# Transformer layer on one core: the start of the attention re-ordered, query weights in two loads, a third weight buffer and later weight differences

## What is computed

```python
x = x + attention(layernorm(x))      # 32 heads of 16, 8 key/value heads
x = x + ffn(layernorm(x))            # 512 -> 1792 -> 512, silu(gate) * up
# bitnet_linear, for q, k, v and o:
s = maximum(mean(abs(weight), axis=1), 1e-8)
y = einsum('bsi,oi->bso', x, sign(weight / s[:, None])) * (s * scale_param)
# weights of the ffn (w1, w2, w3, each with its mean matrix):
d = w - base; W = base + mean(abs(d)) * sign(d)
```

## Time and profile before

| | us |
|---|---|
| median of three runs | 1043.14 |
| lowest and highest run | 1037.54, 1047.61 |
| the profiled execution, its own time | 1045.2 |
| its span, first to last instruction | 1043.4 |

### The profile page before, as it was taken

How to read it: one execution, slowest core, us unless ns; L and a number is a source line. 1 busy time by engine, 2 the same in 40 slices (tenths; PEclk the granted TensorE clock), 3 DMA queues, 4 the chain that set the end, 5 groups by cost and what they waited for, 6 DMA issues and landing times.

```text
span 1043.4 us, 14700 instructions
## 1 busy us (share of the span) xinstructions
PE 967.9 (93%) x4962; PEld 625.4 (60%) x4962; DVE 712.9 (68%) x946; ACT 553.3 (53%) x1078; POOL 301.7 (29%) x310
## 2 busy tenths in 40 slices
PE   6478989999989998898789999999999999999997
PEld 5233443344334433333457888888888888888886
DVE  4666878689978796685785558845686457864443
ACT  4436878888888887784673322233213232232231
POOL 3455537654665432324401110101101111111110
PEclk8768989999999998898999999999999999999999
DMA  5417557467645676632383000340003300220001
GB/s 181 136 26 207 149 146 198 146 195 186 201 121 157 186 190 180 201 98 83 103 291 127 1 1 1 106 141 0 0 0 123 123 0 0 69 93 0 0 0 41
DMA packets 77684, 109.74 MB, mean 105 GB/s; under 512 B 6720, under 2 KB 30272, under 8 KB 77632
## 3 DMA queue, kind: packets, MB, share of 16 engines
q1 hardware_dynamic: 76768, 108.09, 34.4%
q10 hardware_dynamic: 416, 0.66, 0.2%
q0 software_dynamic: 448, 0.33, 0.2%
HBM read 75.17 MB, written 32.77 MB: 103 GB/s over the span
## 4 chain that ended last, share of the span: by engine, by line
PE 72%; POOL 7%; DVE 5%; DMA 4%; issue 4%; SPq 4%; ACT 3%; ACTq 0%; DVEq 0%; POOLq 0%
PE psum L1597 15%; PE psum L1598 15%; PE psum L1599 15%; PE psum L1501 7%; PE psum L1491 6%; PE psum L1475 4%; PE psum L1395 3%; DMA stage<-in_L_ffn_mean_w_dram 2%; PE psum L1396 2%; POOL xn L693 2%; PE psum L1512 1%; PE psum L1513 1%; DVE stage L1309 1%; POOL stage L757 1%; DVE nmx L1147 1%
## 5 line engine op out<-in xcount | busy, mean ns | idle before, releaser
L1147 DVE TENSOR_REDUCE nmx<-psum 128x2 f32<-128x1024 f32 x256 | 305.0, 1221 | 84.9 <-PE psum L1475 82.5
L975 ACT ACTIVATE probs<-psum 128x512 f32<-128x512 f32 x512 | 270.6, 600 | 57.6 <-PE psum L1491 57.1
L1597 PE MATMUL psum<-fxh,wh 128*128 128x512 f32 x448 | 175.3, 391 | 2.2 <-DVE wl L1320 2.2
L837 POOL CAST dh<-w2T 128x512 fp32r<-128x512 f32 (+1 forms) x56 | 50.8, 909 | 430.7 <-PE psum L1599 393.6
L1598 PE MATMUL psum<-fxl,wh 128*128 128x512 f32 x448 | 175.0, 391 | 0.0
L1599 PE MATMUL psum<-fxh,wl 128*128 128x512 f32 x448 | 174.9, 391 | 0.0
L1491 PE MATMUL psum<-q_slot,k_slot 50*128 50x512 f32 x512 | 155.4, 485 | 18.1 <-ACT probs L975 13.7
L1491 PEld LDWEIGHTS psum<-q_slot,k_slot 50*128 50x128 f32 x512 | 67.4, 192 | 139.0 <-ACT probs L975 69.7
L1501 PE MATMUL psum<-probs,v_slot 128*32 128x512 f32 x1024 | 144.3, 637 | 0.0
L1327 DVE TENSOR_TENSOR gate<-gate,psum 128x512 f32<-128x512 f32 x56 | 38.4, 686 | 133.8 <-PE psum L1599 131.5
L1033 ACT ACTIVATE hh<-gate 128x512 fp32r<-128x512 f32 x56 | 35.4, 632 | 162.2 <-DVE gate L1327 162.2
(11 more groups left out here) (133 smaller groups left out, 1315.7 us busy)
## 6 DMA issues: line engine op xcount, KB each, us to landing
stage<-in_L_ffn_mean_w_dram SPq DMA_DIRECT2D x84, 256.0 KB, 4.4
q_slot<-q_stack SPq DMA_DIRECT2D x62, 192.0 KB, 3.3
stage<-in_L_ffn_w_dram SPq DMA_DIRECT2D x42, 256.0 KB, 5.2
q_stack<-q_hi SPq DMA_DIRECT2D x32, 256.0 KB
weighted_values<-u_sb SPq DMA_DIRECT2D x32, 256.0 KB, 3.9
k_slot<-k_stack SPq DMA_DIRECT2D x62, 96.0 KB, 3.6
q_stack<-q_lo SPq DMA_DIRECT2D x16, 256.0 KB
an<-weighted_values SPq DMA_DIRECT2D x16, 256.0 KB
```

Of the source, the lines that this page charges most:

```text
L837: nc.gpsimd.tensor_copy(dh[parity][:], w2T[:, bass.ds(src, 1), :].rearrange("p o c -> p (o c)")).then_inc(dh_ok, 1)
L975: nc.scalar.activation(probs[kt][:, j, :], BANK[ring_bank(("score", g, kt, j))], ACT.Exp, scale=HEAD_DIM ** -0.5).then_inc(exp_ok, 1)
L1147: v.tensor_reduce(column, pair, AX.X, ALU.max, negate=True).then_inc(s_max, 1)
L1597: mm(o, lhs_hi, rhs_hi, start=first, stop=False)
```

## The change

The tiles of K, V and Q are renumbered so that K, V and the first quarter of Q come together. The query weights arrive in two loads, the first quarter alone. The scales of K, V and that quarter are made at once. ACT's magnitudes and signs of the other quarters move behind the first items. PE multiplies the K item as each quarter of `xl` is ready. Twelve small loads of group 0 go over SP and ACT and six over POOL; before it was eight and ten. The third and fourth quarter of Q's pieces are placed one by one after plain scores 2 to 12, the four output sign tiles after 7 to 10. Tile 0 of the differences is loaded in the prologue, ahead of group 1. `stage` gets a fifth buffer, w uses three of the five and mean two, magnitudes overwrite w's buffer. Differences, statistics, `NORM_AT` and `ATTENDED_AT` shift by a few slices, `PROJECT_AT` comes two slices earlier, and five mean tiles are loaded ahead in the last five groups. Renamed indices and the unchanged body of `load_tile` are cut from the diff.

```diff
-QT, KTILE, VTILE, OT = 0, 4, 5, 6
+KTILE, VTILE, QT, OT = 0, 1, 2, 6
...
-LATER = (None, 3, 0, 0)
-XT_AT, SPLIT_AT, STATS_AT, AGGR_AT = 0, 1, 14, 18
-NORM_AT = (24, 26, 28, 30)
+LATER = (None, 2, 0, 0)
+XT_AT, SPLIT_AT, STATS_AT, AGGR_AT = 0, 1, 18, 22
+NORM_AT = (24, 25, 27, 28)
...
-SELECT_AT = (2, 7)
-INVERT_AT, ATTENDED_AT = 27, 9
-PROJECT_AT = (22, 24, 26, 28)
+SELECT_AT = (6, 11)
+INVERT_AT, ATTENDED_AT = 27, 12
+PROJECT_AT = (20, 22, 24, 26)
...
-DIFF_AT = tuple(range(5, 112, 8))
+DIFF_AT = tuple(range(8, 113, 8))
...
-RING = 4
+RING, RING_HERE = 5, 4
...
-    stage = [mid(f"stage{p}", [P, 3, HID]) for p in range(RING)]
-    wn, mn = stage[0::2], stage[1::2]
+    stage = [mid(f"stage{p}", [P, 3, HID]) for p in range(RING_HERE)]
...
-    mid("below_late", [P, 1280])
+    stage.append(mid("stage4", [P, 3, HID]))
+    wn, mn = stage[0::2], stage[1::2]
...
-    WEIGHT_SETS = ((KTILE, 2), (QT, 4), (OT, 4))
+    WEIGHT_SETS = ((KTILE, 3), (QT + 1, 3), (OT, 4))
...
-    FIRST_LOADS, FIRST_POOL = 8 * 16, 10 * 16
+    FIRST_LOADS, FIRST_POOL = 12 * 16, 6 * 16
...
-    TOTALS_SLICE, MEANS_SLICE, COEFF_SLICE = 119, 120, 121
+    TOTALS_SLICE, MEANS_SLICE, COEFF_SLICE = 121, 122, 123
...
-    def first_keys(eng, part):
+    def first_keys(eng, part, done):
...
-            eng.dma_start(k_slot[0][r:r + HEAD_DIM, :].bitcast(FP32), src[0:HEAD_DIM].bitcast(FP32)).then_inc(first_in, 16)
+            eng.dma_start(k_slot[0][r:r + HEAD_DIM, :].bitcast(FP32), src[0:HEAD_DIM].bitcast(FP32)).then_inc(done, 16)
...
+        def load_difference(e, part):
+            if part == 0:
+                if e >= 3:
+                    sp.wait_ge(facc_ok, 3 * (e - 2))
+                    sp.wait_ge(fsgn_ok, 3 * (e - 2))
+                load_tile(e, wn[e % 3], (w1, w3, w2), fw_in[e % 3])
+            else:
+                if e >= 2:
+                    sp.wait_ge(fd_ok, 3 * (e - 1))
+                load_tile(e, mn[e % 2], (m1, m3, m2), fw_in[e % 3])
...
-        sp.dma_start(w_nat[:, QT:QT + 4, :], q_w.rearrange("(t p) c -> p t c", p=P)).then_inc(w_in[1], 16)
+        sp.dma_start(w_nat[:, QT, :], q_w[0:P, :]).then_inc(w_in[1], 16)
+        sp.dma_start(w_nat[:, QT + 1:QT + 4, :], q_w.rearrange("(t p) c -> p t c", p=P)[:, 1:, :]).then_inc(w_in[2], 16)
...
-        sp.dma_start(w_nat[:, OT:, :], o_w.rearrange("(t p) c -> p t c", p=P)).then_inc(w_in[2], 16)
+        sp.dma_start(w_nat[:, OT:, :], o_w.rearrange("(t p) c -> p t c", p=P)).then_inc(w_in[3], 16)
...
+        sp.wait_ge(qh_ok, 1)
+        first_keys(sp, 1, slot_in[0])
+        first_keys(sp, 2, slot_in[0])
...
+        load_difference(0, 0)
+        load_difference(0, 1)
...
-        def load_difference(e, part):
-            if part == 0:
-                if e >= 2:
-                    sp.wait_ge(facc_ok, 3 * (e - 1))
-                    sp.wait_ge(fsgn_ok, 3 * (e - 1))
-                load_tile(e, wn[e % 2], (w1, w3, w2), fw_in[e % 2])
-            else:
-                load_tile(e, mn[e % 2], (m1, m3, m2), fw_in[e % 2])
...
-            if g == 0:
-                load_difference(0, 0)
-                load_difference(0, 1)
-            elif g % 2 == 1 and g // 2 + 1 < IT:
+            if g % 2 == 1 and g // 2 + 1 < IT:
...
-            elif g % 2 == 0 and g // 2 < IT:
+            elif 0 < g // 2 < IT and g % 2 == 0:
...
-            if g >= GROUPS - 4:
-                e = g - GROUPS + 4
-                sp.wait_ge(facc_ok, 3 * (IT - 1 + e // 2))
-                sp.wait_ge(fsgn_ok, 3 * (IT - 1 + e // 2))
+            if g >= GROUPS - RING:
+                e = (4, 1, 0, 3, 2)[g - GROUPS + RING]
+                last = (IT - 3, IT - 2, IT - 2, IT - 1, IT - 1)[g - GROUPS + RING]
+                if e in (1, 3):
+                    sp.wait_ge(fd_ok, 3 * (last + 1))
+                else:
+                    sp.wait_ge(facc_ok, 3 * (last + 1))
+                    sp.wait_ge(fsgn_ok, 3 * (last + 1))
...
-        pool.wait_ge(qh_ok, 1)
-        first_keys(nc.gpsimd, 1)
-        first_keys(nc.gpsimd, 2)
...
-        first_keys(nc.gpsimd, 0)
+        first_keys(nc.gpsimd, 0, first_in)
...
-        for part in range(2):
-            first_heads(nc.gpsimd, part, 1, first_in)
+        first_heads(nc.gpsimd, 1, 1, first_in)
+        pool.wait_ge(ql_ok, 2)
+        first_heads(nc.gpsimd, 2, 1, first_in)
+        for t in range(2):
+            norm_tokens(1, t)
...
+        norm_tokens(1, 2)
+        split_item(0, 3)
...
-        split_item(0, 3)
+        norm_tokens(1, 3)
...
-        for t in range(TT):
-            norm_tokens(1, t)
...
-                pool.wait_ge(fw_in[e % 2], 96 * (e // 2 + 1))
-            nc.gpsimd.tensor_tensor(wn[e % 2][:, k, :], wn[e % 2][:, k, :], mn[e % 2][:, k, :], ALU.subtract).then_inc(fd_ok, 1)
+                pool.wait_ge(fw_in[e % 3], 96 * (e // 3 + 1))
+            nc.gpsimd.tensor_tensor(wn[e % 3][:, k, :], wn[e % 3][:, k, :], mn[e % 2][:, k, :], ALU.subtract).then_inc(fd_ok, 1)
...
+        act.wait_ge(w_in[1], 16)
+        magnitude(QT)
...
-        for m in (KTILE, VTILE):
+        for m in (KTILE, VTILE, QT):
...
-        act.wait_ge(w_in[1], 16)
-        for m in range(QT, QT + 4):
-            magnitude(m)
-        for m in (KTILE, VTILE):
+        for m in (KTILE, VTILE, QT):
...
-        act.wait_ge(wstat_ok, 2)
-        sign_tile(QT)
...
-        signs_out(QT)
...
-        sign_tile(QT + 1)
+        act.wait_ge(w_in[2], 16)
+        magnitude(QT + 1)
+        magnitude(QT + 2)
...
-        sign_tile(QT + 2)
+        magnitude(QT + 3)
...
+        act.wait_ge(qh_ok, 2)
+        first_heads(act, 0, 1, slot_in[0])
...
-        for jj in range(2):
-            first_heads(act, 2, jj, slot_in[0])
-        signs_out(QT + 1)
+        first_heads(act, 2, 0, slot_in[0])
...
-        signs_out(QT + 2)
-        sign_tile(QT + 3)
-        signs_out(QT + 3)
+        act.wait_ge(wstat_ok, 2)
+        for m in (QT + 1, QT + 2, QT + 3):
+            sign_tile(m)
+        for m in (QT + 1, QT + 2, QT + 3):
+            signs_out(m)
+        act.wait_ge(w_in[3], 16)
+        for m in range(OT, WTILES):
+            magnitude(m)
+        act.wait_ge(oscale_ok, 2)
...
-        act.wait_ge(w_in[2], 16)
-        for m in range(OT, WTILES):
-            magnitude(m)
-        scale_item(0, 4, 4)
...
+        scale_item(0, 4, 4)
+        for m in range(OT, WTILES):
...
-                    nc.scalar.activation(mn[e % 2][:, k - 3, :], wn[e % 2][:, k - 3, :], ACT.Abs,
+                    nc.scalar.activation(wn[e % 3][:, k - 3, :], wn[e % 3][:, k - 3, :], ACT.Abs,
...
-            dve.wait_ge(abs_ok, (2, 6, 10)[n])
+            dve.wait_ge(abs_ok, (3, 6, 10)[n])
...
-        weight_scales(1)
...
-        output_scales(slice(0, OT))
+        output_scales(slice(KTILE, QT + 1))
...
+        guard(1)
...
-        guard(1)
...
+        weight_scales(1)
+        output_scales(slice(QT + 1, OT))
...
-        guard(2)
...
+            if nn == 1:
+                guard(2)
...
-            if nn == 8:
+            if nn == 9:
...
-        output_stats(TT - 1)
...
-        def project_item(b, i, bank, half=None):
+        def project_item(b, i, bank, half=None, first=False):
...
+                if first:
+                    pe.wait_ge(xl_ok, kt + 1)
...
-        for m in (KTILE, VTILE):
+        for m in (KTILE, VTILE, QT):
...
-        transpose_signs(QT)
-        pe.wait_ge(signs_ok, 1)
-        for kt in range(KT):
-            pe.wait_ge(xl_ok, kt + 1)
-        first_item(0)
...
+        project_item(0, 0, 4, first=True)
...
-        transpose_signs(QT + 1)
-        transpose_signs(QT + 2)
-        pe.wait_ge(signs_ok, 4)
-        first_item(3)
-        def output_signs():
-            pe.wait_ge(v_ok, 1)
-            for m in range(OT, WTILES):
-                transpose_signs(m)
-            pe.wait_ge(oscale_ok, 2)
+        for m in (QT + 1, QT + 2, QT + 3):
+            transpose_signs(m)
+        def output_factors():
+            pe.wait_ge(oscale_ok, 3)
...
-            if nn == 1:
-                transpose_signs(QT + 3)
-                pe.wait_ge(signs_ok, 5)
+            if nn == 2:
+                pe.wait_ge(signs_ok, OT)
+                first_item(3)
+            if nn == 4:
...
-            if nn == 3:
-                pe.wait_ge(signs_ok, OT)
+            if nn == 6:
...
-            if nn == 6:
-                output_signs()
-            if nn == 8:
+            if 7 <= nn < 11:
+                pe.wait_ge(v_ok, 1)
+                transpose_signs(OT + nn - 7)
+            if nn == 9:
...
-            if nn == 9:
+            if nn == 11:
+                output_factors()
+            if nn == 12:
...
```

More of the change, by code:

```diff
@@ L448, in group_stored, with load_tile @@
                 sp.wait_ge(part_out[(5 * b + i) % Q_RING], stored(b, i))
+        def load_tile(e, dst, sources, done):
+            for k in range(2):
+                sp.dma_start(dst[:, k, :], sources[k][bass.ds(e * P, P), :]).then_inc(done, 16)
```

(39 more changed lines are left out.)

7 lines of the change are left out of this document (3 added, 4 removed).

## The result

| | before | after |
|---|---|---|
| median of the runs | 1045.38 us (4 runs, 1037.54 to 1048.86) | 1005.72 us (4 runs, 1000.96 to 1006.73) |
| span of the profiled execution | 1043.4 us | 1004.2 us |

The ratio is 0.9622, with a 95% interval from 0.9556 to 0.9687: 3.8% faster. The forecast was 998, with 984 to 1023 as its range.

A forecast was written before the change was run, and what follows sets the result against it. PE bounds the last 495.4 us, a constant; before that, waits and order can move. Prologue 12, batch 0 14, batches 1 and 2 7, batch 3 8, weight stage 6: 47 us off 1045.2 gives 998, range 984 to 1023.

The forecast's parts named there:

- Inside the batches: Attention batches 0 to 2: stalls from late data and order go, 14 us less in batch 0, 7 in 1 and 2.
- Rival A: Batches and weight stage: stalls are only handed on to DVE's or ACT's order, half comes back; 1015 us, chance 0.22.
- Prologue: Up to slice 0: earlier items, first plain score at 32 us, slice 0 at 55.3; 12 us less.
- rival C: Whole kernel: more goes than counted and the clock stays up, prologue gaining another 2 to 4 us; 987 us, chance 0.11.
- The cover: Prologue, ninth score: the sign copies cover up to 2 us of wait for group 1's load.
- that sum: Prologue under the shared DMA engines rule: wait for group 1 nearer 5 us, saving 9 us instead of 12.
- Batch 3: Last attention batch: reciprocals' stall goes, means matmul and projections move; 8 us less.
- The failed step: Batch 3: one projection moves to a slice with plain scores, costing at most 0.6 us.
- Weight stage: After the last batch: first load 3.6 us sooner, one tile fewer to load 2.4 us; 6 us less.

The follow-up runs named there:

- experiment 10: Kernel before plus only the third w buffer, differences from slice 8 and totals two slices later, ring of four: 1021.22 us median, 0.980 of before.
- experiment 5: Changed kernel with the differences three slices earlier again, from slice 5, third buffer kept: 1016.8 us median.
- experiment 7: Changed kernel with POOL's normalisations back at slices 24, 26, 28, 30: 1003.28 us, one run.
- experiment 1: Changed kernel with the loads of difference tile 0 moved behind group 2's load: 1005.83 us median.
- experiment 8: Changed kernel with the query weights in one load of 1 MB again: 1012.7 us median.
- experiment 3: Changed kernel with `ATTENDED_AT` back at 9 instead of 12: 1009.54 us, one run.
- experiment 2: Changed kernel with the four projections put back to slices 118, 120, 122 and 124: 1001.33 us median.
- experiment 6: Changed kernel with a ring of four tiles in the weight stage instead of five: 1003.47 us, one run.
- the last two variants: Changed kernel with DVE's selection between the two maxima and projections at (20, 22, 26, 28), 996.14 us; the same with tile 0's difference load behind group 2's, 991.97 us.
- experiment 9: Changed kernel unaltered, 1005.13 us; with selection between the maxima and projections at (20, 22, 26, 28), 996.14; with the difference load late too, 991.97.
- the variant with two and two projections: Changed kernel with DVE's selection between the two maxima and projections at slices 116, 118, 122 and 124: 996.14 us median.

## Why the prediction held, step by step

**Inside the batches: right, in mechanism and size.** For batch 0, 14 of 17.0 us were forecast and 14.8 measured; for batches 1 and 2, 7 and 7.6. The differences alone give 11.3, 4.4 and 5.2 us (experiment 10); moved back in the changed kernel they cost 11 us in the median (experiment 5). The remaining stall of batch 0 stands in experiment 10 at 8.15 us, and the changed kernel's interval there is 3.3. That the statistics of batch 2's tokens, one slice later now, take it away fits DVE's wait of 3.1 us for these tokens in experiment 10, but this part was not tested alone. The normalisations' new places are nothing (experiment 7), as the step had it: the wait between them was the cause. Rival A, that the stalls are handed on, didn't come in batches 0 to 2; that DVE's order takes the place of POOL's waits came at the end of batch 3, through the moved projection.

**Prologue: right about the path, one term too small, and partly luck.** The second `q_hi` came at 24.2 (25 forecast) and the first plain score at 31.2 (32). K's item gained less than I had it: its output was taken at 20.0 instead of 22.7, 2.7 us and not 3.8, since PE's 16 token transposes took 3.34 us at a low clock, behind the sign transpose that I had called hidden. That `q_hi` was on time all the same is luck: I had reckoned with the clock of before, 0.73 from 18.8 to 29.0, and the items ran at 1.00 (17.4 to 24.0). Over the whole prologue the granted clock was 0.78 instead of 0.76, so rival C's clock gain came in the items and not beyond them. From the first score to slice 0, 23.3 us were forecast and 28.0 measured, and 4.1 of these are the wait for group 1, which I had put at up to 2 us and covered. The cover, ACT's copies of signs, was not there: ACT itself waited 3.75 us for PE. My own estimate put the load's issue at 42 (41.24) and its landing at 47; the keys were there only at 48.4. The measured wait is near the 5 us that the prediction had estimated from the rule of the Trainium skill (DMA: Bandwidth & Descriptors, Issuing engines are not separate DMA queues) that all transfers share the same 16 DMA engines, and the prologue's 8.5 us near the 9 of that sum; the page gives no time for it. The traces agree with the rule in kind: without the 1.5 MB in front the rows took 5.2 and 5.4 us from issue to score instead of 6.4 to 7.5. About 2 us of wait remain even then, because the issue itself waits for the stores (experiment 1), which my sum did not name. The split load carried more than its place in my sum, 4 to 6 us (experiment 8).

**Batch 3: the step that failed.** Its first half did what was said, 8.4 us, and experiment 3 brings the stall back. The failed step is: one of the projections "moves from a slice without plain scores to one with them, at most 0.6 us." The stretch grew by 7.4 us; with the projections put back it is 7.1 us shorter (experiment 2). I had priced the projection by PE's work alone. A projection in a slice with plain scores also needs a PSUM bank that DVE empties after two maxima and the selection of the one before. After such a wait the granted clock was 0.50 (440 to 445 us), and the third projection's eight products took 3.8 us where the second one's took 2.1 at 1.00; around the third one, the two intervals are 7.4 and 6.7 us. Before, two projections stood there and PE waited 2.9 us in all for `oy`; after, three and 6.9 us.

**Weight stage: right, a little large.** Of 6 us forecast, 4.9 came. PE's first transpose came right behind the copy of the last values, and the fifth tile gave 1.1 to 1.7 us instead of 2.4 (experiment 6). One wait there is not for loads: DVE waited 4.3 us for ACT's high part of the normalised tokens, in the changed kernel and in that of experiment 6 alike.

**What stays open:** where the 4.2 us between the medians of the last two variants lie, what each of the smaller shifts in batch 0 is worth alone, and why PE's token transposes begin at the low clock in some executions and not in others.

## What to carry to other kernels

Where an in-order engine waits for a transfer, ask what is queued behind it: here POOL's wait for a late 1.5 MB load reached PE through the engines behind POOL, and using the data three slices later, with one more buffer, was worth about 20 us of 1041 (experiment 10). Price a moved matmul not by its own time alone but by who empties its PSUM bank and what stands ahead of that in the emptying engine's order; that was the step that failed here, and a better order of DVE and of the projections gave 9 us (experiment 9). A large load that is not urgent belongs behind the small ones that are, even if its issue looks hidden: it lengthened the small ones' transfer by about 2 us without delaying their issue.

## What was not expected of the hardware

A wait of little more than 1 us inside a busy stretch can cost several. In the kernel of experiment 2, PE waited 1.3 us for a small load of shift rows in batch 1, and the granted clock then was:

```profile
245.00:250.00 5.00, 5.00 (x34) 2.07 (x33) 4.76 (x7) 4.43 (x10) 5.00 (x4) 1.00 0.79 203
250.00:255.00 5.00, 3.69 (x24) 1.65 (x16) 2.88 (x3) 3.10 (x7) 4.44 (x4) 0.69 0.83 227
255.00:260.00 5.00, 5.00 (x24) 1.64 (x16) 2.90 (x3) 3.81 (x9) 0.24 (x1) 0.50 0.59 196
260.00:265.00 5.00, 4.96 (x29) 2.36 (x25) 3.55 (x5) 3.49 (x8) 1.28 (x1) 0.79 0.34 77
```

At 0.50, 1.2 GHz, PE is busy for the whole 5 us and does 24 matmuls instead of 34. Batch 1 took 105.4 us there and 101.0 in the changed kernel, whose own such place, a wait of 1.35 us, was in batch 2 and cost less: 102.1 us, where experiment 6 had 100.3. This is probably part of why runs of one kernel lie 10 us and more apart: of the eleven runs of before on the chip of experiment 9, the shortest, 1035.72 us, had a mean granted clock of 0.964, and the longest, 1048.67, 0.950.

The start is another place where the clock differs from run to run. PE's token transposes of batch 0, in the changed kernel (granted clock 0.57 from 12.9 to 16.3 us) and in the variant with two and two projections, whose start is the same (1.00):

```profile
12.92 3.34 PE L1431 MATMUL psum<-ident,xn 128*128 128x128 f32 x16
```

```profile
12.32 1.92 PE L1432 MATMUL psum<-ident,xn 128*128 128x128 f32 x16
```

With the 0.6 us by which they begin earlier, these are the 2 us between a first plain score at 31.2 and one at 29.2.
